# Two token groups in the expert stages, with all second matrices on chip and addressed by a register

## What is computed

```python
x = _layernorm(x + _L0_attn_ref(x, ...))      # stage A
x = _layernorm(x + _L0_xattn_ref(x, ctx, ...))  # stage B
x = _layernorm(x + _L0_ffn_ref(x, ...))        # stage C: experts, 2 of 8 per token, F = 512, gelu
x = _layernorm(x + _L1_attn_ref(x, ...))       # stage D
x = _layernorm(x + _L1_xattn_ref(x, ctx, ...))  # stage E
x = _layernorm(x + _L1_ffn_ref(x, ...))        # stage F: experts, 1 of 8 per token, F = 256, relu

# an expert stage, for each token and each expert e that it chose
h = jax.nn.relu(jnp.einsum('td,edh->teh', tokens, W1) + b1[None])
y = jnp.einsum('teh,ehd->ted', h, W2) + b2[None]
```

## Time and profile before

| what | value |
|---|---|
| three runs | 1644.38, 1647.92, 1642.45 us; median 1644.38 |
| the profiled execution | 1640.13 us |
| its span in the profile | 1638.3 us |
| granted TensorE clock, mean share | 0.912 |
| busy: PE, PEld, DVE, ACT, POOL | 1328.1, 743.1, 854.0, 831.8, 546.9 us |
| DMA | 67.30 MB, mean 41 GB/s |
| scatters and gathers on POOL | 158 indirect DMAs |

### The profile page before, as it was taken

The page is one execution under the profiler, slowest core; times in us unless marked ns, Lnnn a source line. Parts: engine busy times, 40 slices in busy tenths (PEclk is TensorE's granted clock), DMA queues, the critical chain, the costliest instruction groups (busy, mean ns, idle before and its releaser), DMA issues.

```text
span 1638.3 us, 22200 instructions
## 1 busy us (share of the span) xinstructions
PE 1328.1 (81%) x6934; PEld 743.1 (45%) x6934; DVE 854.0 (52%) x2721; ACT 831.8 (51%) x1885; POOL 546.9 (33%) x511
## 2 busy tenths in 40 slices
PE   5999999999999888876549658788889897796460
PEld 2434434444443345444248636455555554444250
DVE  3444543453344354674522176777666775557525
ACT  4777677677677535453225345446454552343130
POOL 3455455455445411323454342100000110112253
PEclk9999999999999989987769879889999997887685
DMA  9000000000000000000259600000000000000172
GB/s 371 23 1 1 1 1 1 1 1 1 1 1 1 1 0 1 1 1 13 85 187 339 222 26 9 6 1 1 1 1 1 1 1 0 1 1 7 37 234 59
DMA packets 35074, 67.30 MB, mean 41 GB/s; under 512 B 5424, under 2 KB 21296, under 8 KB 33808
## 3 DMA queue, kind: packets, MB, share of 16 engines
q1 hardware_dynamic: 29328, 54.37, 9.6%
q0 software_dynamic: 5056, 10.36, 2.1%
q10 hardware_dynamic: 576, 1.16, 0.2%
HBM read 47.71 MB, written 18.15 MB: 40 GB/s over the span
## 4 chain that ended last, share of the span: by engine, by line
PE 60%; DVE 19%; issue 8%; ACT 5%; DMA 5%; POOL 2%; DVEq 0%; ACTq 0%; POOLq 0%
PE bank L503 8%; PE bank L485 7%; PE bank L493 6%; PE bank L432 5%; DMA work<-xs,xi 4%; PE bank L608 3%; PE bank L806 3%; PE bank L475 3%; PE bank L565 3%; PE bank L579 3%; PE bank L802 2%; DVE work L1321 2%; PE bank L594 1%; PE bank L672 1%; POOL xs L1866 1%
## 5 line engine op out<-in xcount | busy, mean ns | idle before, releaser
L1813 POOL TENSOR_TENSOR work<-work 128x512 f32<-128x512 f32 x256 | 266.5, 1041 | 277.6 <-DVE work L1329 277.6
L944 ACT ACTIVATE work<-bank,work 128x512 f32<-128x512 f32 x256 | 176.5, 689 | 117.8 <-DVE work L1321 117.6
L1321 DVE TENSOR_REDUCE work<-bank 128x1 f32<-128x512 f32 x256 | 176.7, 690 | 76.7 <-PE bank L485 75.8
L493 PEld LDWEIGHTS bank<-cst,work 128*128 128x128 f32 x1024 | 110.5, 140 | 164.4 <-issue 106.0
L493 PE MATMUL bank<-cst,work 128*128 128x128 f32 x1024 | 160.0, 283 | 6.6 <-ACT work L952 6.1
L1329 DVE RECIPROCAL work<-work 128x1 f32<-128x1 f32 x256 | 41.9, 164 | 222.6 <-ACT work L944 222.3
L952 ACT ACTIVATE work<-bank 128x512 f32<-128x512 f32 x256 | 152.6, 596 | 0.5 <-PE bank L493 0.5
L1914 POOL TENSOR_TENSOR work<-work 128x512 f32<-128x512 f32 x32 | 40.9, 1277 | 332.4 <-PE bank L806 312.6
L485 PE MATMUL bank<-work 64*128 64x512 f32 x512 | 144.5, 641 | 3.4 <-ACT work L944 3.4
L1853 POOL TENSOR_TENSOR work<-work 128x1232 f32<-128x1232 f32 (+1 forms) x32 | 55.5, 1735 | 250.3 <-DVE work L1401 250.2
L503 PE MATMUL bank<-work 128*64 128x512 f32 x512 | 137.4, 617 | 0.7 <-ACT work L952 0.7
(11 more groups left out here) (232 smaller groups left out, 2550.0 us busy)
## 6 DMA issues: line engine op xcount, KB each, us to landing
W<-in_wC SPq DMA_DIRECT2D x39, 578.0 KB
xs<-gat SPq DMA_DIRECT2D x9, 1024.0 KB, 16.5
W<-in_wF SPq DMA_DIRECT2D x23, 321.0 KB
ys<-work SPq DMA_DIRECT2D x62, 64.0 KB
x_all<-in_x SPq DMA_DIRECT2D x4, 256.0 KB, 8.7
W<-in_L_attn_Wq SPq DMA_DIRECT2D x2, 512.0 KB, 5.5
W<-in_L_attn_Wv SPq DMA_DIRECT2D x2, 512.0 KB, 7.6
W<-in_L_attn_Wo SPq DMA_DIRECT2D x2, 512.0 KB, 9.0
```

Of the source, the lines that this page charges most:

```text
L493: m = nc.tensor.transpose(out[:, k * P:(k + 1) * P], pA[u % 5][:, k * P:(k + 1) * P], ident)
L944: A(pA[u % 5], bank[u % 3][:, :], ACT.Exp, bias=nmax[:, u % 8:u % 8 + 1], accum_out=rsum[0][:, u % 8:u % 8 + 1]).then_inc(sem("a_e"), 1)
L1321: V.tensor_reduce(nmax[:, u % 8:u % 8 + 1], bank[u % 3][:, :], AX, ALU.max, negate=True)\
L1813: G.tensor_tensor(pA[u % 5], pA[u % 5], rsum[1][:, u % 8:u % 8 + 1].to_broadcast([P, S]), ALU.mult)\
```

## The change

The tokens of an expert stage are split in two groups: batches 0 to 2 (`NG = 3`) and batch 3. Each has its own sorted lists, DRAM tensors (`xs0`, `xs1`, `ys0`, `ys1`), map and places. The tiles of group 0 begin as soon as batch 2 is ranked; the tail of the last unit, the routing of batch 3, its scatters and the map of group 1 now stand between the tiles, at the steps of new tables `STEPS`, `POOL_STEPS` and `TAIL[2]`, `TAIL[5]`. The bound of tiles is taken for each group: 31 + 15 in C, 19 + 11 in F. The y of batch 0 of C is gathered at tiles 41 to 44 and the batch closed at step n of the loop.

The second matrices of all eight experts (2 MB in C, 1 MB in F) are loaded once into the upper half of `W0`; the per-tile load holds the first matrix and the biases alone (330 KB, 193 KB) in one of six buffers. TensorE reads the tile's expert number into a register and takes the second matrix at that address. There are six buffers for gathered rows instead of three and three for their transposes instead of two; `moe_h` stands two steps behind the transpose and `moe_y` four. The scatters of batch 0 in the cross stages are issued in four parts, at steps 15 to 18.

```diff
+NG = 3
+CAPS = (NG * S, (NB - NG) * S)
+def tile_bound(k):
+    return [(k * c + E * (P - 1)) // P for c in CAPS]
+TILES0, TILES1 = tile_bound(2), tile_bound(1)
-NW = 7
-WIDE = FT0 * 2 * P + FT0 + P
-WIDE1 = FT1 * 2 * P + FT1 + P
+NX = 6
+NW = 6
+WIDE = FT0 * P + FT0 + P
+WIDE1 = FT1 * P + FT1 + P
...
+        STEPS = {2: (13, 14, 15, 16, 17, 18, 19), 5: (7, 8, 9, 11, 12, 13, 14)}
+        POOL_STEPS = {2: (8, 21, 41), 5: (0, 15, 99)}
...
...

+                w2 = W0[:, 4096:4096 + E * m_["ft"] * P]
+                sp.dma_start(v3(w2, E), T[m_["w"] + "2"]).then_inc(dma_in["w2"], 16)
+                for j in range(n):
...
...
             def moe_h(m_, j):
...
+                chosen[J] = pe.value_load(em[0:1, j:j + 1], min_val=0, max_val=E - 1)
                 pe.wait_ge(sem(f"M_w{J % NW}"), 16 * (J // NW + 1))
                 pe.wait_ge(sem("M_xT"), J + 1)
...
             def moe_y(m_, j):
                 J, ft = m_["j0"] + j, m_["ft"]
+                e, w2 = chosen[J], v3(W0[:, 4096:4096 + E * ft * P], E)
                 pe.wait_ge(sem("M_h"), J + 1)
...
-                    m = mm(out[:, 0:D], hTM[J % 3][:, f * P:(f + 1) * P], wM[J % NW][:, (ft + f) * P:(ft + f + 1) * P],
+                    m = mm(out[:, 0:D], hTM[J % 3][:, f * P:(f + 1) * P], w2[:, bass.ds(e, 1), f * P:(f + 1) * P],
...
                 moe_logits(m_, 2)
-                tail(m_["w0"] - 1, 0)
                 moe_prefix(m_, 2)
-                for s in range(1, 5):
-                    tail(m_["w0"] - 1, s)
-                moe_logits(m_, 3)
-                moe_prefix(m_, 3)
-                n = m_["tiles"]
-                for j in range(n + 3):
+                tail(w, 0)
+                n = sum(m_["tiles"])
+                for j in range(n + 4):
                     if j < n:
                         moe_turn(m_, j)
-                    if 1 <= j <= n:
-                        moe_h(m_, j - 1)
-                    if j >= 3:
-                        moe_y(m_, j - 3)
+                    tail(w, j + 1)
+                    if j == at[0]:
+                        moe_logits(m_, 3)
+                    if j == at[3]:
+                        moe_prefix(m_, 3)
+                    if 2 <= j < n + 2:
+                        moe_h(m_, j - 2)
+                    if j >= 4:
+                        moe_y(m_, j - 4)
...
...
+                moe_map(m_, 0)
+                moe_places(m_, 0)
+                for j in range(n + 4):
...
+                    tail(w, j + 1)
+                    if j == at[1]:
+                        moe_route1(m_, 3)
+                    if j == at[2]:
+                        moe_route2(m_, 3)
+                    if j == at[4]:
+                        moe_rank(m_, 3)
+                    if j == at[5]:
+                        moe_map(m_, 1)
+                    if j == at[6]:
+                        moe_places(m_, 1)
+                    if ph == 2 and j == n:
+                        close_x(m_, 0)
...
...
-                    if u == 15:
-                        moe_scatter(MOE[ph + 1], 0)
+                    if 15 <= u < 19:
+                        moe_scatter(MOE[ph + 1], 0, u - 15)
...
+                    if j == own:
+                        tail(m_["w0"] - 1, tail_steps(m_["w0"] - 1)[2])
+                    if put <= j < put + NT:
+                        moe_scatter(m_, 3, j - put)
+                    if get <= j < get + NT:
+                        moe_gather(m_, 0, j - get)
```

More of the change, by code:

```diff
@@ L389, in moe_weights @@
-                for j in range(m_["tiles"]):
+                n = sum(m_["tiles"])
+                w2 = W0[:, 4096:4096 + E * m_["ft"] * P]
+                sp.dma_start(v3(w2, E), T[m_["w"] + "2"]).then_inc(dma_in["w2"], 16)
+                for j in range(n):
                     J = m_["j0"] + j
+                    if j == 0:
+                        sp.wait_ge(sem("M_map"), m_["g0"] + 1)
+                    if j == m_["tiles"][0]:
+                        sp.wait_ge(sem("M_map"), m_["g0"] + 2)
+                    if m_["n"] == "F" and j == -m_["j0"] % NW:
+                        sp.wait_ge(y_ready, yn(PF))
@@ L1095, in moe @@
                 ft = m_["ft"]
+                w, at = m_["w0"] - 1, STEPS[ph]
                 moe_exp(m_, 2)
-                for s in range(5):
-                    tail(m_["w0"] - 1, s)
-                moe_exp(m_, 3)
+                tail(w, 0)
                 enter(act, ph)
-                for j in range(m_["tiles"]):
-                    J = m_["j0"] + j
+                n = sum(m_["tiles"])
+                for j in range(n + 2):
+                    tail(w, j + 1)
+                    if j == at[1]:
+                        moe_exp(m_, 3)
+                    if j < 2:
+                        continue
+                    J = m_["j0"] + j - 2
                     act.wait_ge(sem("M_hp"), J + 1)
@@ L1535, in moe_map, with moe_places @@
                                             op0=ALU.mult, op1=ALU.subtract))
-                V.scalar_tensor_tensor(out=xi[:, 0:n], in0=row[:, 0:n], scalar=float(P), in1=const("slot")[:, 0:n],
+                V.scalar_tensor_tensor(out=xi[:, j0:j0 + n], in0=row[:, 0:n], scalar=float(P), in1=const("slot")[:, 0:n],
                                        op0=ALU.mult, op1=ALU.add).then_inc(sem("M_xi"), 1)
+            def moe_places(m_, g):
+                K = m_["k"]
+                first = g * NG * NT * K
+                every = (NB - NG if g else NG) * NT * K
@@ L1550, in moe @@
+                n, ft = sum(m_["tiles"]), m_["ft"]
                 moe_rank(m_, 1)
@@ L1879, in moe @@
             def moe(ph):
                 m_ = MOE[ph]
-                moe_scatter(m_, 1)
-                for s in range(5):
-                    tail(m_["w0"] - 1, s)
-                moe_scatter(m_, 2)
-                moe_scatter(m_, 3)
+                own, put, get = POOL_STEPS[ph]
+                K, done = m_["k"], 2 * NB * NT * (m_["b0"] // NB)
+                for b in (1, 2):
+                    for t in range(NT):
+                        moe_scatter(m_, b, t)
                 enter(pool, ph)
-                pool.wait_ge(sem("M_xi"), m_["b0"] // NB + 1)
@@ L1895, in moe @@
-                pool.wait_ge(sem("M_gi"), m_["b0"] // NB + 1)
-                for i in range(3):
-                    pool.wait_ge(sem(f"M_ys{i}"), 16 * len(range(i, m_["j0"] + m_["tiles"], 3)))
-                for b in range(2 if ph == 2 else NB):
-                    moe_gather(m_, b)
+                    if j == 0:
+                        pool.wait_ge(sem("M_xi"), m_["g0"] + 1)
+                        pool.wait_ge(sem("M_sc"), 16 * (done + NG * NT * K))
+                    if j == m_["tiles"][0]:
+                        pool.wait_ge(sem("M_xi"), m_["g0"] + 2)
+                        pool.wait_ge(sem("M_sc"), 16 * (done + NB * NT * K))
@@ L1901, in phase_d @@
+                    if get <= j < get + NT:
+                        moe_gather(m_, 0, j - get)
+                if ph == 2:
+                    for t in range(NT):
+                        moe_gather(m_, 1, t)
+                else:
+                    for b in range(NB):
+                        for t in range(NT):
+                            moe_gather(m_, b, t)
             def phase_d():
@@ L1909, in phase_d @@
                     if g in (1, 5):
-                        moe_gather(MOE[2], 2 + g // 5)
+                        for t in range(NT):
+                            moe_gather(MOE[2], 2 + g // 5, t)
                     pool.wait_ge(sem("d_el"), g + 1)
```

234 lines of the change are left out of this document (130 added, 104 removed).

## The result

The changed kernel took 1675.0 us (median of 4 runs, 1673.98 to 1679.95), the kernel before 1645.16 us beside it. The ratio is 1.0187, with a 95% interval of 1.0160 to 1.0214: slower, where the prediction had 1611 us. Its span is 1672.2 us, 33.9 longer.

What follows compares the result with a forecast made beforehand. TensorE and DMA were both taken as full in C's tile loop, with waits around it. C -15.1 and F -14.4 us, together -29.5 from 1640.13, gave 1611 us; own range 1600 to 1625, whole range 1588 to 1648.

Steps and rivals of the forecast that it cites:

- 1 and 2, scatters and early start: Batch 0's scatters split: softmax blocks 7.6 and 3.6 us earlier; first x gather 29.3 us earlier in C, 18.7 in F.
- its rival (delays of later blocks): For the split scatters alone: half the gain taken back by delays of later blocks, leaving 0.2 to 0.4%.
- 3, more tiles: Padded tiles: 46 for 39 in C, 30 for 23 in F; fewer bytes per tile take DMA off the path.
- step 4: C's tile on TensorE: 1.90 us if register work is hidden, 2.84 if it adds in full; took 2.35.
- Rival (a): Register work on TensorE is hidden, C's tile at 1.90 us, 20.7 us less: 1590 us; chance 0.27.
- step 5: C's loop, first gather to last y: 121.8 us for 87.2, +34.6; GpSimd's 83 us fit inside.
- VectorE's routing pieces are covered: In C's loop: VectorE's routing pieces stand between tiles and three x buffers cover them; no time added.
- 6, handover: From C's last y to the next stage's first transposed x: 3 us instead of 23.5, -20.4.
- 7, F: F's loop 54.9 us for 41.9, +13.0, at 1.52 us a tile; closings start at the last y, -8.7.
- (c): TensorE's granted clock falls to 1.2 GHz in C, tile at 3.6 us, +58: 1668 us; chance 0.12.
- (b): Register work on TensorE adds in full, C +22.5 and F +7.5 us: 1641, no change; chance 0.16.
- (d): Early start doesn't come, scatters or gathers late beside weights, 10 us lost: 1621 us; chance 0.07.

Runs made afterwards that it cites:

- split_alone: Kernel before with only the scatters of batch 0 split over four steps of the cross-attention; ratio 0.9973 (0.995 to 1.000).
- paced_b: Changed kernel with three x buffers, batch 3's scatters one a tile, no y gathers in loops; ratio 1.0087, in its earlier run (paced) 1.009.
- the third run: Changed kernel, unaltered, measured again beside later edits; ratio 1.0223, loop of C 151.7 us.
- the first series: Four edits of the changed kernel, each taking suspects away, run before the unaltered change was repeated; ratios 0.992, 0.999, 1.008 and 1.009.
- fixed_second: Changed kernel, but TensorE reads no expert number and always takes expert 0's second matrix at a fixed address; ratio 0.992, repeated later 1.0195.
- late_gathers: Changed kernel, but C's batch 0 gathered and closed after the loop, F's y gathers waiting for all tiles; ratio 1.008, loop of F 64.7 us.
- drained: Changed kernel with three x buffers, GpSimd waiting for each pair of its scatters and y gathers to land; ratio 1.0220, loop of C 147.9 us.

## Why the prediction was wrong, step by step

1 and 2, scatters and early start: nearly right. -26.5 us for -29.3 in C; split_alone measured -0.27% (4.4 us, with an interval of 0.5 to 8.4) where the step had 11.2; its rival (delays of later blocks) was nearer. In F the start came 14.6 us earlier for 18.7.

3, more tiles: right. They aren't free: 46 x 1.90 is 13.3 us more than 39 x 1.90 in each run with two groups.

4, **time of a tile in C, the first wrong size**: 2.35 us predicted, 1.90 measured, since the register work runs wholly beside the array. The changed kernel's L707, about what SyncE's took the earlier trace rows:

```profile
L707 PEldq TENSOR_LOAD <-em x76: 296/302/490, 822.0 to 1640.3; - x76
L707 PEldq FUSED_REGOPS  x76: 146/151/165, 822.5 to 1640.7; - x76
```

The window 905 to 915 has TensorE 10.00 of 10 us busy. That is the lower bound of the step. The page TensorE: Matmul & The Clock Gate of the Trainium skill (spec table: the engine's queue of instructions) leans the right way. The Trainium skill's page DMA: Bandwidth & Descriptors (latency and other measured facts) gives such a load a floor of about 600 ns; these rows show 302, and the measurement decides. Rival (a) had this premise; its 1590 us are further off than the forecast, since the other loss is larger.

5, **the loop of C, the step that failed**: "GpSimd's 46 gathers, 8 scatters, 8 gathers of y and one LayerNorm piece are 62 x 1.27 + 4 = 83 us, less than the loop". I counted GpSimd's time and asked only whether it was less than the loop's. That it runs beside the others without holding them up was taken for granted. In C's loop of before x gathers come one per tile, but F's loop and stage D of before had close transfers, and the delays beside them, and I didn't look there. Steps 5 and 7 were 60.2 us too short, and by step 4 the true gap is larger: at 1.90 us a tile the sum of step 5 was 101.1, so 50 us in C are stops and delays that it didn't have. Thinning brought 34.8 of them back (paced_b against the third run; its closing stands outside the loop, which is some 5 of them). Some 20 us of paced_b remain (116.9 less 97.1, the sum without that closing). paced of the first series, whose trace has no late event, still has 112.4, so about 15 of them aren't delays of this kind; that they are the short pieces of batch 3 on VectorE is likely and not shown ("VectorE's routing pieces are covered" was then too kind). fixed_second, also without a late event, has 118.8 us, near the 121.8 of the step: there the tile predicted too slow and these pieces left out cancel, which would have been luck. The closing of batch 0 held VectorE 7.1 us (955.76 to 962.83), and TensorE waited 5.18 for it, near the 4 predicted.

6, handover: right, 1.9 us left for 3.

7, F: loop +43.8 for +13.0. Stops are most of it. But with the streams thinned it is still 66.3 us for 54.9 predicted: in late_gathers the chain goes through SyncE and a weight load, behind a y add:

```profile
1588.16 0.30 DVE work L1637
1588.48 0.33 SPq L407
1589.01 0.34 SPq L425
...
1592.14 2.67 DMA W<-in_wF
1594.86 0.71 PE bank L712 x4
```

The put and the load of a slot wait for its add, and the landing of 2.67 us isn't hidden by six slots when a tile takes 1.0 us on TensorE at the full clock. SyncE's issue time was counted, the landing wasn't.

The rivals: (c), the slower side at 1668 us, was near the number, but not by its mechanism: the granted clock is 1.00 in the steady loop, and in the long stop it falls after TensorE had begun to wait (1.00 in 920 to 925, 0.56 in 925 to 930). (b) and (d) didn't occur. "The prediction falls if VectorE's pieces hold TensorE for several microseconds each" came true once, by the closing; the main cause stood in no rival.

## What to carry to other kernels

Adding up an engine's issue time shows that it has room, not that its work is free for the others: before a tile loop is given indirect transfers at 1.25 us where it had one per 1.9, look in the trace for a place that already has both. Here stage D and F's loop of the kernel before were such places, and showed "remote" waits of 4.4 and 2.3 us. Try the parts of a change that don't need its costly one: with groups and everything thinned it was still 0.9% slower, while the parts that need no groups gained 0.6%. And run the unaltered change in the same series as each edit of it: two conclusions of mine came from comparing series. When a run with added waits comes out slow, look first at what those waits starve: drained was slow for its own drain.

## What the runs showed of the hardware

- Beside indirect transfers issued every 1.25 us TensorE's semaphores were raised late, and in bunches, in sixteen of twenty profiles: y was seen up to 3.3 us late with four in a row, VectorE waited 12.6 us beside eleven, and in drained's loop, with runs of three or four, no late event was longer than 1.9 us. ScalarE's own were never late. It needs no other transfers beside them and no registers on TensorE. In attention stage D the delays were up to 5.8 us, and TensorE did as many matmuls as in ten microseconds without them (51).
- The four profiles of the first series had the same kind of transfers and no late event; what made the difference isn't known.
- A register load on TensorE takes 302 ns and two register operations 151 and 18 ns; 17 pairs of weight load and matmul at 112 ns cover them with four address computations entirely.
- The size of the stops isn't constant: the same kernel had C's loop at 118.8 us in one series and at 152.1 in another.
